# Graph network on one core: step two's adjacency products in other turns, scores first while the pipeline fills, another end factor in the search

## What is computed

```python
for s in range(2):
    Q, K = Xa @ W1, Xa @ W3
    logits = Q @ W2 @ K.T
    # per row: keep the largest entries until their softmax reaches 0.9
    keep = smallest_set_with_mass(softmax(logits), 0.9)
    A = softmax(where(keep, logits, -inf))
    Xf = Rf @ Xf; Xb = Rb @ Xb; Xa = A @ Xa
    Z = Z + Xf @ U1[s] + Xb @ U2[s] + Xa @ U3[s]
Y = layernorm(X + Z)
# layer 3
out = x + (1 - t) * support + t * (adj @ support)   # support = relu(layernorm(x)) @ weight
```

## Time and profile before

| what | us |
|---|---|
| median of 3 runs (lowest, highest) | 3476.09 (3475.62, 3479.3) |
| the profiled execution, its own time | 3477.54 |
| its span, first to last instruction | 3475.8 |
| TensorE busy | 3141.6 (90%) |
| VectorE busy | 2449.9 (70%) |
| GpSimd busy | 2154.7 (62%) |
| ScalarE busy | 1598.2 (46%) |

### The profile page before, as it was taken

How to read it: one execution, slowest core, us unless ns; L and a number is a source line. 1 busy time by engine, 2 the same in 40 slices (tenths; PEclk the granted TensorE clock), 3 DMA queues, 4 the chain that set the end, 5 groups by cost and what they waited for, 6 DMA issues and landing times. The chain is left out here.

```text
span 3475.8 us, 42043 instructions
## 1 busy us (share of the span) xinstructions
PE 3141.6 (90%) x13212; PEld 2270.6 (65%) x13212; DVE 2449.9 (70%) x3401; ACT 1598.2 (46%) x2357; POOL 2154.7 (62%) x4214
## 2 busy tenths in 40 slices
PE   4999989997799999999976689988899999996899
PEld 3888778885567777777754255544566666664788
DVE  6840123333998889888883799999988999998000
ACT  2311322225666666666653445545555555652100
POOL 2212421114788888888881677878988788886211
PEclk9999999998899999999988899999999999998899
DMA  7644344433112222122111111211222222233255
GB/s 254 241 146 145 116 151 167 165 130 87 44 54 59 61 63 60 57 60 64 57 37 58 47 56 53 57 48 51 58 82 75 78 80 82 74 87 99 96 197 173
DMA packets 140702, 327.59 MB, mean 94 GB/s; under 512 B 15456, under 2 KB 93664, under 8 KB 129248
## 3 DMA queue, kind: packets, MB, share of 16 engines
q1 hardware_dynamic: 140512, 325.30, 29.5%
HBM read 286.70 MB, written 38.54 MB: 94 GB/s over the span
## 5 line engine op out<-in xcount | busy, mean ns | idle before, releaser
L1025 ACT ACTIVATE junk<-E,negp 128x3327 uint8<-128x3327 f32 x208 | 637.3, 3064 | 141.3 <-issue 107.3
L1397 DVE SCALAR_TENSOR_TENSOR U<-E,trial 128x3327 f32<-128x3327 f32 x182 | 678.1, 3726 | 0.0
L920 PE MATMUL bank<-big,adj 128*128 128x512 f32 x1352 | 608.7, 601 | 8.7 <-ACT t L1051 8.7
L920 PEld LDWEIGHTS bank<-big,adj 128*128 128x128 f32 x1352 | 252.4, 192 | 328.9 <-issue 327.9
L297 PE MATMUL bank<-big,E 128*128 128x256 f32 x1664 | 366.7, 382 | 2.8 <-PEq L58 1.7
L880 PE MATMUL bank<-Hc,PT 128*128 128x256 f32 x1248 | 303.1, 395 | 65.5 <-ACT PT L1064 65.4
L880 PE MATMUL bank<-Hc,adj 128*128 128x256 f32 x1456 | 338.0, 384 | 16.4 <-ACT adj L1064 16.2
L297 PEld LDWEIGHTS bank<-big,E 128*128 128x128 f32 x1664 | 315.8, 191 | 50.3 <-issue 5.7
L1359 DVE TENSOR_REDUCE nmax<-E 128x1 f32<-128x3327 f32 x52 | 188.0, 3615 | 208.8 <-ACT E L1068 208.8
L880 PEld LDWEIGHTS bank<-Hc,adj 128*128 128x128 f32 x1456 | 279.5, 193 | 79.8 <-issue 22.5
L880 PEld LDWEIGHTS bank<-Hc,PT 128*128 128x128 f32 x1248 | 244.3, 198 | 126.3 <-ACT PT L1064 77.0
(11 more groups left out here) (248 smaller groups left out, 5750.2 us busy)
## 6 DMA issues: line engine op xcount, KB each, us to landing
adj<-adjT SPq DMA_DIRECT2D x131, 448.0 KB, 3.4
E<-adjT SPq DMA_DIRECT2D x32, 1664.0 KB, 6.9
adj<-adjT SPq DMA_DIRECT2D x104, 384.0 KB, 3.3
adj<-adjT SPq DMA_DIRECT2D x20, 1664.0 KB, 7.0
E<-adjT SPq DMA_DIRECT2D x26, 1216.0 KB, 5.8
xt<-xin SPq DMA_DIRECT2D x52, 128.0 KB, 5.8
x_d<-xn SPq DMA_DIRECT2D x52, 128.0 KB, 1.7
xt<-x_d SPq DMA_DIRECT2D x52, 128.0 KB, 5.3
```

The lines of the kernel that those rows point to most:

```text
L920: last = mm(agg[:, 0:w], adj[:, SPAN * (k % 2) + j - AGG[k]], rhs[:, j], start=(j == 0), stop=False)
L1025: go(junk[:, 0:N], E[:, t % DEPTH, 0:N], func, bias=negp[:, t % 2, j:j + 1], scale=1.0, accum_out=acc_[:, t % 2, j:j + 1]).then_inc(summed ...
L1397: V_.scalar_tensor_tensor(out=U[:, 0:N], in0=e, scalar=point, in1=e, op0=ALU.is_ge, op1=ALU.mult, accum_out=found))
```

## The change

Four edits:

- `LATE` goes from 7 to 5 and `agg_at` gets an exception: the adjacency product of tile 26 is in turn 27, which has no scores, and that of tiles 27 to 51 in turns 32 to 56, the turns in which the same tile's scores are made.
- In turns with scores but without transposes (`filling`: 0 to 3 and 31 to 34) the four adjacency pieces come after all four score pieces, not between them. This holds for step one too.
- The 13 side pairs are in turns 45 to 48, 50 to 52 and 54 to 59 instead of 45 to 57. Where the turn has no adjacency product (57 to 59), SyncE issues the pair's loads on its own (`load_side`). `CLOSE` = 7 keeps the turn of the last loads and the number of tiles stored on the way as they were.
- `KEEP_END` of step two goes from 0.75 to 0.85.

```diff
--- before.py
+++ after.py
@@ -24,7 +24,7 @@
 SHIFT = (1.4, 0.0)
 STEER = (2.0, 4.0)
 AIM = (3.0, 4.0)
-KEEP_END = (0.8, 0.75)
+KEEP_END = (0.8, 0.85)
 RIDGE = (8.0, 4.0)
 QUANTILE = 1.2815515655446004
 DENSITY = 0.17549833193248685
@@ -39,7 +39,9 @@
 AGG = (0, 7, 14, 20, 26)
 DEPTH = 4
 LAG = 5
-LATE = 7
+LATE = 5
+CLOSE = 7
+PAIRS = (0, 1, 2, 3, 5, 6, 7, 9, 10, 11, 12, 13, 14)
 FIRST = 7
 SPAN = 7
 POINT, GAP, GOAL, MASS, BELOW = 0, 1, 2, 3, 4
@@ -683,7 +685,7 @@
             soon = [flat(wkk), flat(wqq), wd[:, 0], wd[:, 1], ua[:, 0, D:2 * D], ua[:, 1, D:2 * D], uc[:, 0, D:2 * D]]
             held = [bias0[:], uc[:, 1, D:2 * D]]
             side_bank = [dense[:, D:2 * D], misc[:, D:2 * D]]
-            side_at = lambda i: i - (NT + LAG + FIRST + 7) if 0 <= i - (NT + LAG + FIRST + 7) < NT // 2 else None
+            side_at = lambda i: PAIRS.index(i - (NT + LAG + FIRST + 7)) if i - (NT + LAG + FIRST + 7) in PAIRS else None
             hT3, h3o, cn3 = ub[:, :, 0:D], ub[:, :, D:2 * D], uc[:, :, 0:D]
             halves = lambda ap: ap.rearrange("p (h c) -> p h c", h=2)
 
@@ -697,13 +699,13 @@
             post_at = lambda i: shown(i - 5)
             first = lambda n: n is not None and n < NT
             second = lambda n: n is not None and n >= NT
-            agg_at = lambda i: i if 0 <= i < NT else i - LATE if NT <= i - LATE < tiles else None
+            agg_at = lambda i: i if 0 <= i < NT else NT if i == NT + 1 else i - LATE if NT < i - LATE < tiles else None
             sent_at = lambda i: agg_at(i - 1)
             norm_at = lambda i: post_at(i - 1) - NT if second(post_at(i - 1)) else None
             last_at = lambda i: post_at(i - 2) - NT if second(post_at(i - 2)) else None
             rounds = NT + LAG + NT + 7
             early = NT - LAG
-            spread = [b for i in range(rounds + 1) for b in [last_at(i)] if b is not None and i < tiles + LATE]
+            spread = [b for i in range(rounds + 1) for b in [last_at(i)] if b is not None and i < tiles + CLOSE]
             kept = len(spread)
             turned = lambda i: sum(first(sent_at(k)) or first(post_at(k)) for k in range(i))
             dense_g = lambda i: sum(first(sent_at(k)) for k in range(i))
@@ -752,6 +754,10 @@
                             to = SPAN * (k % 2)
                             sp.dma_start(adj[:, to:to + j1 - j0], adjT[n % NT, :, j0:j1]).then_inc(adj_in[k], 16)
 
+                        def load_side(v, k):
+                            to = SPAN * k
+                            sp.dma_start(adj[:, to:to + FIRST], adjT[2 * v + k, :, 0:FIRST]).then_inc(side_in[k], 16)
+
                         def load_q(t):
                             src = q0_d[t] if t < NT else kq_d[t - NT, :, P:2 * P]
                             sp.dma_start(qt[:, t % 2], src).then_inc(q_in[t % 2], 16)
@@ -818,9 +824,7 @@
                                     if k < 2:
                                         load_chunk(n, k + 2)
                                     elif v is not None:
-                                        to = SPAN * (k - 2)
-                                        sp.dma_start(adj[:, to:to + FIRST],
-                                                     adjT[2 * v + k - 2, :, 0:FIRST]).then_inc(side_in[k - 2], 16)
+                                        load_side(v, k - 2)
                                     elif n + 1 < tiles:
                                         load_chunk(n + 1, k - 2)
                                 if k == 0 and i >= 1:
@@ -844,10 +848,14 @@
                                 sp.wait_ge(ub_done, NT)
                                 sp.dma_start(w3, Wg3.rearrange("(c p) f -> p c f", p=P)).then_inc(w3_in, 16)
                             if v is not None:
+                                if n is None:
+                                    for k in range(2):
+                                        load_side(v, k)
                                 for k in range(2):
                                     sp.wait_ge(side_done[k], v + 1)
-                                    load_chunk(n + 1, k)
-                            if i == tiles + LATE:
+                                    if n is not None and n + 1 < tiles:
+                                        load_chunk(n + 1, k)
+                            if i == tiles + CLOSE:
                                 for k in range(2):
                                     sp.wait_ge(tr_done, SLOTS * (tiles - 3 + k))
                                     sp.dma_start(square(E[:, k])[:, FIRST:NT], adjT[k, :, FIRST:NT]).then_inc(next_in, 16)
@@ -930,6 +938,7 @@
                         for i in range(rounds):
                             L, T, X = score_at(i), turn_at(i), post_at(i)
                             n, G = agg_at(i), sent_at(i)
+                            filling = L is not None and T is None
                             if X is not None:
                                 values(X, SLOTS - 1)
                             for k in range(SLOTS):
@@ -995,7 +1004,10 @@
                                         pe.wait_ge(xo_copied, NT)
                                     hT = hT3[:, W % 2]
                                     product(dense, [hT[:, c * P:(c + 1) * P] for c in range(DC)], w3, D).then_inc(d3_done, 1)
-                                if n is not None:
+                                if n is not None and not filling:
+                                    neighbours(n, k)
+                            if n is not None and filling:
+                                for k in range(SLOTS):
                                     neighbours(n, k)
                             v = side_at(i)
                             if v is not None:
```

## The result

The changed kernel takes **3496.09 us** (3495.92 to 3496.88, four runs), the kernel before, run beside it, 3475.86. The ratio is 1.0059 with an interval of 1.0047 to 1.0071: slower by 20 us where 18 faster was forecast.

What follows compares the result with a forecast made beforehand. VectorE's search was taken to set step two's pace, with TensorE as the floor under it. The terms +10 + 0 + 15 - 2 + 0 - 41 = -18 from the profiled 3477.5 gave a median forecast of 3458 us, range 3428 to 3508.

Steps and rivals of the forecast that it cites:

- Fill one: Step one's first turns without transposes: scores first, products after, delay the third tile's maximum; +10 us (6 to 14).
- Step change: Turn 27: tile 26's adjacency products fit into TensorE's idle stretches; 0 us (-3 to +4).
- Fill two: Step two's first turns: tile 27's products ahead of turn 33's scores delay tile 28's maximum; +15 us (8 to 18).
- The end: End of step two: the 3.6 us gap before the last search shrinks with fewer GpSimd additions; -2 us (-4 to 0).
- Side pairs: Turns 45 to 56 hold 10 pairs instead of 12: 12.2 us less TensorE, by itself moving nothing; 0 us.
- KEEP_END: Step two's search: factor 0.85 leaves 11 extra top-8 passes instead of 19; -41 us.
- Rival 1: Step two's passes stay at about 19, so only the fills speak: 3499 us, slower; chance 0.20.
- Rival 3: Nearly all extra passes of step two go and TensorE becomes the bound: 3431 us; chance 0.15.
- Rival 4: The fills cost nothing, because ScalarE's list was the bound with or without the products: 3438 us; chance 0.08.
- Rival 2: Five or more extra passes are added, as weaker pull leaves a far end standing: 3544 us; chance 0.10.

Runs made afterwards that it cites:

- the two fill runs: The changed kernel with step one's fill in the old order, 3479.35 us; the changed kernel with no fill 'scores first' and LATE 6, 3464.89 us.

## Why the prediction was wrong, point by point

- **Fill one, +10 (6 to 14): 15.1, and 16.7 of the end time.** Mechanism right, size above my bound (13.9 in the trace of the changed kernel with 0.75, whose fill is the same). Most of the miss is in the sum "some 9 us later": the third turn's scores started at 842.16 instead of 829.21, 13.0 later, since each of the two turns before grew by 6.5. The first took 24.7 (791.35 to 816.06), at the upper end of my 22 to 25, the second 26.1 instead of 24.5, with waits for the exp and for loads. The rest is the ScalarE chain that "does not shorten": it grew. From the end of its first score piece, 842.16+1.13, to the maximum at 863.26 are 20.0 us, against 848.17-830.34 = 17.8 before.
- **Step change, 0 (-3 to +4): 0.2.** The idle stretches took tile 26's products as worked out.
- **Fill two, +15 (8 to 18): 12.8 in the trace, 13.0 by the pair of traces (10.1 in the trace of 0.75).** Block and identity product took 24.8 us (I had 26.1), and ScalarE's list behind it 1940.1 to 1957.0 = 16.9 (17.6). Both terms held.
- **The end, -2:** held: with 19 extra passes the schedule takes the gap of 3.6 to 1.0; that GpSimd's fewer additions do it is not shown. In the changed kernel itself it is 0.1 for another reason, tile 50's pass. **Side pairs, 0:** no run moves them alone. In the trace of 0.75, with the passes of the kernel before, the lateness falls from 23.5 us at the end of tile 26's search to 17.9 at the end of tile 51's; 2.6 of these 5.6 are the gap, the rest is not told apart.
- **KEEP_END, -41:** this is the step that failed, twice over. It brought 3.0 here, and the 38 us missing are as much as the whole forecast was off (20.2 against -18). *The count:* 17 extra passes, not 11. The step treated the values near the cut as scattered singles, "scatter of the values adds about sqrt(ab/(a+b))". The rows that fail have equal values there, and a better trial point can't separate them: two more evaluations leave 14 of 19, making the values unequal leaves 1. *The price:* I let 41 of 72 us through for eight passes, 5.1 each, with TensorE's floor as the only other bound. All 19 of step two together bring 42.6 in the traces. On average the runs give 2.3 us a pass (22 passes, 50.3 us) and 2.2 (18 passes, 39.7 us); the first two bring 3.8 each in the kernel before (7.6) and 1.5 in the changed one (3.0). No run has eight passes fewer; at 2.2 to 3.8 the term would have been an estimated -18 to -30 and the sum +5 to -7, hardly a forecast of a gain. In the turns with side pairs I gave 13 us for 3 to 4 passes, and seven of them brought 0.9. In the turns before them I missed GpSimd, because I judged it by its mean, 37.1 of 48.9 us, and did not read its timeline for gaps and long operations.
- **The rivals.** Rival 1 (3499, passes stay) is what happened. That it is only 3 us off is partly luck: fill one cost 7 more than it had, and the two spare passes, fill two and the end gave 3, 2 and 5 back. Its price of 5 us a pass was too high, and its "from about 4 fewer passes downward" with it. Rival 3 (3431 with nearly no extra passes) falls: the changed kernel with none in either step takes 3459. Rival 4 falls by the two fill runs. Rival 2 (more passes) is real at 0.95, where they come in a heap, but not at 0.85.
- **The sum with what was measured:** +16.7 (fill one) +13.0 (fill two) +0.2 (step change) -3.0 (factor in this schedule) leaves 26.9; the remaining -6.7 to the measured 20.2 goes with the 5.6 by which the lateness falls towards the end without any help from the passes.

## What to carry to other kernels

While a pipeline fills, small work interleaved on one engine is cover for the waits of another; putting it behind in one block adds both lengths, and the first wait at the far end shows it at full price. Before a step is credited with fewer rounds of a data-dependent loop, look at which data keep it open: equal values need another remedy than a better start. And a round saved is worth 9 us only while its engine sets the pace: read every engine's timeline in a turn with the fewest rounds, since one at 89% with gaps of at most 0.2 us is full. The first round saved and the last are not worth the same.

## What the runs showed of the hardware

- A GpSimd operation on 128x1 to 128x4 values takes 0.2 to 0.6 us and at other times 3.6 to 3.8, and one of 128x256 values 0.72 or 4.0 to 4.1 us. All 48 long ones of eight turns started during an operation of VectorE that reads two rows of 3327 elements; of the 233 that started during MAX8, MATCH_REPLACE8 or a maximum over one such row none was long.
- A phase with gaps costs clock as well. Windows of TensorE in turns 0 and 1 of the changed kernel (stretch, us, busy, clock, DMA, GB/s): idle, scores with waits, the first 28 products, the same 28 one turn later; then turns 31 and 32, scores with waits.

```profile
786.00:791.30 5.30, 0.00 (x0) 0.50 0.61 198
791.30:801.50 10.20, 6.94 (x16) 0.50 0.01 2
801.50:809.70 8.20, 8.20 (x30) 0.76 0.17 48
829.35:835.66 6.31, 6.31 (x30) 1.00 0.21 62
...
1894.50:1904.00 9.50, 5.20 (x19) 0.84 0.70 237
1904.00:1915.20 11.20, 6.17 (x16) 0.50 0.54 170
```

Behind an idle stretch of 8.3 us the scores run at 1.2 GHz, and the clock rises to 2.4 within the first products: 8.19 us for what takes 6.31 in the next turn. In turns 31 and 32 it stood at 2.4 and falls during the scores, with waits of 1.0 to 2.8 us between them.
